# Four graph layers on one core: another order of the node tiles

## The chip, the cores and the metric

The kernel runs on 1 core of one Trainium2 chip. The metric is the device time of one execution in microseconds; before the change it is 1249.79 us, the median of three runs (1248.19 to 1251.66). TensorE is called PE below, VectorE DVE, ScalarE ACT, GpSimd POOL, and SyncE, which only issues DMAs, SP.

## What is computed

Four layers over a graph of 3327 nodes with 512 features. The adjacency matrix is random with about four edges per node, so a layer needs few rows for each node. Each layer adds its result to x:

```python
h = jnp.maximum(_layernorm(x, axis=-1), 0.0)
x = x + _L0_gnn_ref(h, ...)   # relu of [h W_self + b, (mean of the neighbours' h) W_nb + b] W_comb + b
h = jnp.maximum(_layernorm(x, axis=-1), 0.0)
x = x + _L1_gnn_ref(h, ...)   # 8 heads of 64: softmax over the neighbours of leaky_relu(f_src + f_dst), times Wh
h = jnp.maximum(_layernorm(x, axis=-1), 0.0)
x = x + _L2_gnn_ref(h, ...)   # 4 heads of 128 (quaternion weights), then elu
h = jnp.maximum(_layernorm(x, axis=-1), 0.0)
x = x + _L3_gnn_ref(h, ...)   # one head of 512
```

## The kernel before

A first stage (the first quarter of the time) reads the adjacency matrix, makes for each node a list of up to 16 neighbours, counts them, and computes layer 0's projected rows into the DRAM table `T[0]`. It then ranks the nodes by their number of neighbours, most first, and from there on works on tiles of 128 nodes of that ranking. Tile t therefore needs a fixed number of gathered rows for every node of it, `SLOTS[t]`: 15 for tile 0, 8 for tile 1, 7, 7, 6, 6, 6 for tiles 2 to 6, 5 for 7 to 10, 4 for 11 to 15, 3 for 16 to 20, 2 for 21 to 24 and 1 for tile 25, which has 127 nodes; 119 in all. ("A tile with fifteen rows" is meant in this sense; "a row" below is one gathered row for each of the 128 nodes, one indirect DMA.)

`ORDER` (L35) is the order in which every layer goes through the 26 tiles; s is a tile's place in it. All engines run the same order, each its own program:

- POOL (`rows_of`, L1072) issues one indirect DMA per row (L1081) into a ring `GB` of 32 slots. `places` (L89) gives out the slots: it starts again at slot 0 when a tile doesn't fit behind the last one. A slot is written again only when its old row was used (`wait_used`), and tile s waits besides for tile s-8, whose gather semaphore it takes. In layer 0 POOL also gathers each tile's residual row (L1096), in layer 3 it scatters the finished tile to the output (L1111), eight tiles behind the gathers.
- Layer 0: DVE adds the rows of a tile one by one (L1313), each add on the one before, and adds the residual (L1316), round by round, with the norm of the tile before taken between the adds.
- Layers 1 and 2, DVE (L1411): in round r it finishes tile r-3 (L1399 or L1407), normalizes the weights of tile r-1, multiplies that tile's rows with them (`weigh`, L1380; in layer 1 part of the rows are added in pairs, L1392), and takes the first steps of tile r's softmax (`shifted`, L1339 to L1351) and of tile r-3's norm in between. The instructions are in one fixed order, so a wait for tile r's rows at L1339 holds up everything behind it. PE adds the weighed rows of a tile in PSUM with an identity (L703), one sum for each entry of `units`: 94 in layer 1, 119 in layer 2. In PE's round r these sums of tile r-1 alternate with the four steps of tile r-4's projection (L679) in layer 1; what is left over follows behind.
- Layer 3, DVE (L1432): `shifted` of tile r, then the blending of tile r-1 in SBUF (L1460, L1458), each step on the one before; PE transposes the blended tile (L616) and multiplies it with the weights (L749), ACT copies between (L792); DVE adds the product to x (L1440) in round r+3.
- ACT applies the norm (L779), copies the transposed tile to SBUF (L795), takes the exponentials (L845), and copies the projected rows out (L860, L861); SP stores them to the next table (L562).

A node's neighbours may be in any tile, so a layer's first gather waits until the last row of the layer before is stored. `STEP_OF_LAST` is the place of tile 25, the last one in both orders.

Of the kernel before, what the change touches and what calls it, by code (L numbers as in the profile page):

```python
# [31 lines left out]
TILES_WITH = [26, 25, 21, 16, 11, 7, 4, 2, 1, 1, 1, 1, 1, 1, 1]  # L32
SLOTS = [sum(t < n for n in TILES_WITH) for t in range(NT)]
TOTAL = sum(SLOTS)
ORDER = [t for pair in zip([24, 23, 22, 21, 20, 19, 18, 17, 16, 15, 14, 13], [1, 2, 3, 4, 0, 5, 6, 7, 8, 9, 10, 11]) for t in pair] + [12, 25]  # L35
FIRST = [sum(SLOTS[t] for t in ORDER[:s]) for s in range(NT + 1)]
NS = 32

# [3 lines left out]
def units(l, t):  # L42

    pairs = PAIRS[SLOTS[t]] if l == 1 else 0
    return [(2 * k, 2) for k in range(pairs)] + [(k, 1) for k in range(2 * pairs, SLOTS[t])]


def units_ahead(l, s):

    return sum(len(units(i, t)) for i in range(1, l + 1) for t in (ORDER if i < l else ORDER[:s]))  # L50

# [37 lines left out]
def places():  # L89

    base, before, held, at = {}, {}, [None] * NS, 0
    for l in range(4):
        for s, t in enumerate(ORDER):
            if at + SLOTS[t] > NS:
                at = 0
            base[l, s] = at
            for k in range(SLOTS[t]):
                before[l, s, k] = held[at]
                held[at] = (l, s, k)
                at += 1  # L100
    return base, before
# [239 lines left out]
def edges(nc, ctx, g, dr):  # L341
# [85 lines left out]
    BASE, BEFORE = places()  # L427
    STEP_OF_LAST = ORDER.index(NT - 1)
    SETUP = dict(ident=2, xpad=3, mark=7, eight=8, start=9, rowid=10, id=12, upper=14, mrow=16, ones=17, we=18, ones16=19, classes=20, line=21,
# [17 lines left out]
    def wait_gather(e, l, s):  # L447

        e.wait_ge(S[f"gather{s % 8}"], 16 * (l * sum(SLOTS[t] for t in ORDER[s % 8::8]) + sum(SLOTS[t] for t in ORDER[s % 8:s + 1:8])))

    def wait_used(e, l, s, k):
# [4 lines left out]
        elif l < 3:  # L456
            e.wait_ge(S["summed"], units_ahead(l, s) + max(i for i, (first, _) in enumerate(units(l, ORDER[s])) if first <= k) + 1)
        else:
# [1084 lines left out]
```

## Time and profile before

| | |
|---|---|
| median of the runs | 1249.79 us |
| the profiled execution | 1243.5 us, span 1241.8 us |
| PE busy | 897.9 us (72% of the span) |
| DVE busy | 874.3 us (70%) |
| POOL busy | 689.2 us (56%) |
| ACT busy | 394.1 us (32%) |
| chain that ended last | PE 29%, DVE 25%, POOL 16%, DMA 13%, issue 11%, ACT 5% |
| costliest single line of the chain | POOL L1081, the row gathers, 12% |

Busy time is that of an engine over the whole span, not of the path. The chain is what ended last at each moment, followed back from the end; "issue" is time in which an engine waited for nothing that the profile shows. In the time lines a number in brackets is the engine's idle time just before the instruction, with what ended it. A group's mean over the whole run hides that the layers have different limits, so the rows below are of single stretches.

### The profile page before, as it was taken

To read this page: it belongs to the slowest core of one execution; us is meant where nothing else is said; L and a number is where in the kernel's file an instruction comes from. 1 tells how busy PE (TensorE), PEld (TensorE's weight loads), DVE (VectorE), ACT (ScalarE), POOL (GpSimd) and SP (SyncE) were. 2 spreads that over 40 slices of the span, in tenths; PEclk is the share of its full clock that TensorE was granted. 3 is DMA by queue.
4 is the path that set the end of the run, shared out by engine and by line. 5 is a ranking of instruction groups with operands and counts; after the bars stand their busy time and mean duration, and the time that the engine had idled before them with its cause. 6 is when DMAs were issued, how large, how long until landed. Compare 5 with 4: busy or idle time off the path is not lost.

```text
span 1241.8 us, 12157 instructions
## 1 busy us (share of the span) xinstructions
PE 897.9 (72%) x2804; PEld 485.2 (39%) x2804; DVE 874.3 (70%) x2811; ACT 394.1 (32%) x1200; POOL 689.2 (56%) x648
## 2 busy tenths in 40 slices
PE   3985969999256476755999999477888834738674
PEld 1332434444044365542656666234444332313231
DVE  3867699930187698836999897088999945746563
ACT  3552656632023133321323333134354430101110
POOL 4043423365477777617777710377777007777772
PEclk9997989999679689896999999878888966968988
DMA  9999868722678688726757720366677116646662
GB/s 361 387 346 366 316 251 328 224 72 76 200 234 248 181 271 263 238 95 185 202 162 206 209 80 35 95 175 177 188 212 211 53 52 175 171 139 182 181 184 86
DMA packets 81447, 242.74 MB, mean 195 GB/s; under 512 B 16931, under 2 KB 19395, under 8 KB 77275
## 3 DMA queue, kind: packets, MB, share of 16 engines
q0 software_dynamic: 47488, 144.09, 40.1%
q1 hardware_dynamic: 33882, 97.82, 21.4%
q8 instruction: 24, 0.39, 0.1%
q14 instruction: 53, 0.43, 0.1%
HBM read 203.00 MB, written 53.64 MB: 207 GB/s over the span
## 4 chain that ended last, share of the span: by engine, by line
PE 29%; DVE 25%; POOL 16%; DMA 13%; issue 11%; ACT 5%; POOLq 1%; SPq 0%; ACTq 0%
POOL arena L1081 12%; PE psum L679 9%; PE psum L703 7%; PE psum L638 7%; DVE arena L1380 4%; DVE arena L1313 4%; DMA arena<-XV,arena 4%; DVE arena L1192 2%; ACT arena L795 2%; DMA arena<-T,arena 2%; DMA arena<-in_adj 2%; DMA arena<-in_L_gnn_a 2%; DVE arena L1130 2%; DVE arena L1282 2%; PE psum L749 1%
## 5 line engine op out<-in xcount | busy, mean ns | idle before, releaser
L1081 POOL DMA_INDIRECT arena<-T,arena x476 | 518.9, 1090 | 332.9 <-issue 180.3
L703 PE MATMUL psum<-arena,misc 128*128 128x512 f32 x426 | 229.1, 659 | 62.8 <-DVE arena L1380 46.6
L679 PE MATMUL psum<-arena 128*128 128x264 f32 (+1 forms) x832 | 221.1, 412 | 47.3 <-ACT arena L795 47.3
L638 PE MATMUL psum<-arena 128*128 128x512 f32 (+1 forms) x416 | 200.3, 624 | 28.8 <-ACT arena L808 16.4
L679 PEld LDWEIGHTS psum<-arena 128*128 128x128 f32 (+1 forms) x832 | 163.3, 201 | 122.6 <-ACT arena L795 72.3
L616 PE MATMUL psum<-misc,arena 128*128 128x128 f32 (+1 forms) x520 | 87.9, 295 | 145.7 <-ACT arena L779 78.3
L1380 DVE TENSOR_TENSOR arena<-arena 128x512 f32<-128x512 f32 x238 | 160.6, 686 | 1.8
L616 PEld LDWEIGHTS psum<-misc,arena 128*128 128x128 f32 (+1 forms) x520 | 65.4, 152 | 195.8 <-ACT arena L779 89.6
L703 PEld LDWEIGHTS psum<-arena,misc 128*128 128x128 f32 x426 | 82.1, 209 | 146.8 <-issue 100.2
L779 ACT ACTIVATE arena<-arena 128x512 f32<-128x512 f32 x104 | 84.4, 811 | 155.2 <-DVE arena L1289 146.5
L749 PE MATMUL psum<-arena 128*128 128x512 f32 (+1 forms) x208 | 113.2, 695 | 17.9 <-ACT arena L792 17.9
L638 PEld LDWEIGHTS psum<-arena 128*128 128x128 f32 (+1 forms) x416 | 77.7, 198 | 115.0 <-issue 114.0
L1192 DVE FIND_INDEX8 arena<-arena 128x8 uint32<-128x674 f16 x130 | 108.7, 854 | 0.0
L845 ACT ACTIVATE arena<-arena 128x16 f32<-128x16 f32 (+7 forms) x78 | 17.4, 223 | 263.7 <-DVE arena L1351 263.5
L1313 DVE SCALAR_TENSOR_TENSOR arena<-arena 128x512 f32<-128x512 f32 x119 | 88.8, 746 | 16.6 <-DMA arena<-XV,arena 15.5
L1339 DVE TENSOR_TENSOR arena<-arena 128x16 f32<-128x16 f32 (+7 forms) x78 | 14.1, 181 | 118.8 <-DMA arena<-T,arena 118.8
L825 ACT ACTIVATE arena<-arena 128x3330 f16<-128x3330 int32 x26 | 77.4, 2976 | 60.9 <-DVE arena L1192 41.8
L795 ACT ACTIVATE arena<-psum 128x128 f32<-128x128 f32 (+1 forms) x312 | 82.2, 286 | 15.1 <-PE psum L616 15.1
L860 ACT ACTIVATE arena<-psum 128x528 f32<-128x528 f32 (+1 forms) x52 | 31.4, 605 | 133.8 <-PE psum L679 133.8
L749 PEld LDWEIGHTS psum<-arena 128*128 128x128 f32 (+1 forms) x208 | 43.6, 220 | 72.7 <-issue 48.0
L1458 DVE SCALAR_TENSOR_TENSOR arena<-arena 128x512 f32<-128x512 f32 x93 | 70.0, 753 | 1.1
L1130 DVE TENSOR_SCALAR arena<-arena 128x1 f32<-128x1 f32 x234 | 63.6, 272 | 6.8
(138 smaller groups left out, 1006.6 us busy)
## 6 DMA issues: line engine op xcount, KB each, us to landing
arena<-in_adj SPq DMA_DIRECT2D x25, 1663.5 KB, 8.5
T<-arena SPq DMA_DIRECT2D x75, 260.0 KB, 3.6
arena<-T,arena POOLq DMA_INDIRECT x476, 3.8
T<-arena SPq DMA_DIRECT2D x25, 256.0 KB, 2.6
XV<-arena SPq DMA_DIRECT2D x25, 256.0 KB, 2.3
PW<-arena POOLq DMA_DIRECT2D x5, 1024.0 KB, 8.3
arena<-in_x SPq DMA_DIRECT2D x1, 3072.0 KB, 17.6
XV<-arena SPq DMA_DIRECT2D x1, 3072.0 KB, 23.0
```

The lines of the kernel that those rows point to most:

```text
L616: last = e.transpose(p_t[:, k * P:k * P + n], src[0:n, k * P:(k + 1) * P], ident[0:n, 0:n])
L638: last = e.matmul(p_own[which][0:n, :], HT[t % 2][:, k, 0:n], W0[which][:, k, :], start=k == 0, stop=k == 3 and which == 0)
L679: last = e.matmul(p_wh[0:n, a, :], ht[:, k, 0:n], WL[l][:, k, a, :], start=k == 0, stop=k == 3)
L703: e.matmul(p_num[s % 3].rearrange("p (a o) -> p a o", a=2), ident, halves(GB[:, BASE[l, s] + of[n][0], :])[:, :, 0:HALF], start=n == 0, st ...
L749: last = e.matmul(p_num[s % 3][0:n, :], HT[m % 2][:, k, 0:n], W0[0][:, k, :], start=k == 0, stop=k == 3)
L779: e.activation(to[0:n, 0:D], X[0:n, t, :], ACT.Relu, bias=shift[0:n, :], scale=scale[0:n, :]).then_inc(S["h"], 1)
L795: last = e.activation(ht[:, k, 0:n], p_t[:, k * P:k * P + n], ACT.Copy, accum_out=HS[:, k, t:t + 1])
L1081: e.indirect_dma_start(GB[:, BASE[l, s] + k, 0:ROW], None, dr["T"][l], bass.IndirectOffsetOnAxis(ap=(IDP if l else IDX)[:, t, k:k + 1], ax ...
L1130: chain(e.tensor_scalar(t, hv, y, y, ALU.mult, ALU.mult))
L1192: picked = e.max_index(PICK[:, s * 8:s * 8 + 8], EIGHT, MARK[t % 2][:, s * PART:(s + 1) * PART])
L1313: added(e.scalar_tensor_tensor(y, GB[:, base + k, 0:D], SHARE[:, t, k:k + 1], y if k else xv[:, 0:D], ALU.mult, ALU.add))
L1380: return e.tensor_tensor(both, both, p, ALU.mult)
```

## The change

Only the constant `ORDER` changes. `FIRST`, the places in the ring, the gather semaphores (s modulo 8) and every engine's program follow from it; the first stage does not use it.

```diff
-ORDER = [t for pair in zip([24, 23, 22, 21, 20, 19, 18, 17, 16, 15, 14, 13], [1, 2, 3, 4, 0, 5, 6, 7, 8, 9, 10, 11]) for t in pair] + [12, 25]
+ORDER = [24, 23, 22] + [t for pair in zip([1, 2, 3, 4, 5, 6, 7, 8, 9, 10], [21, 20, 19, 18, 17, 16, 15, 14, 13, 12]) for t in pair] + [0, 11, 25]
```

In rows per tile the order is, before and after:

```
before 2 8 2 7 2 7 2 6 3 15 3 6 3 6 3 5 3 5 4 5 4 5 4 4 4 1
after  2 2 2 8 2 7 3 7 3 6 3 6 3 6 3 5 4 5 4 5 4 5 4 15 4 1
```

Tile 0 has slots 9 to 23 of the ring before, and 13 to 27 after.

## Rows read from the trace of the kernel before

**Rows 1.** Groups by line, POOL, stretches 323:521 (first two) and 1021:1211

```profile
L1081 POOL DMA_INDIRECT arena<-T,arena x119 | 126.3, 1062 | 60.6 <-issue 58.1 <-DVE arena L1313 2.4
L1096 POOL DMA_INDIRECT arena<-XV,arena x26 | 27.6, 1060 | 7.9 <-issue 6.7 <-DVE arena L1313 0.9 <-DVE arena L1316 0.3
...
L1081 POOL DMA_INDIRECT arena<-T,arena x119 | 128.7, 1082 | 95.2 <-DMA T<-arena 59.2 <-issue 35.0 <-DVE arena L1460 0.6
```

**Rows 2.** Stretches: length, PE, PEld, DVE, ACT, POOL busy (count), PE clock, DMA, GB/s

```profile
323.60:551.60 228.00, 133.72 (x538) 100.17 (x538) 165.74 (x466) 66.26 (x288) 153.95 (x146) 0.85 0.72 220
...
643.40:766.90 123.50, 115.56 (x424) 73.13 (x423) 114.41 (x410) 41.18 (x191) 58.73 (x53) 1.00 0.49 145
...
823.70:1007.60 183.90, 151.90 (x512) 80.07 (x513) 172.97 (x609) 79.46 (x343) 109.47 (x97) 0.89 0.55 160
...
1021.70:1229.00 207.30, 130.09 (x312) 56.35 (x312) 122.21 (x353) 20.89 (x52) 155.65 (x144) 0.83 0.57 167
```

**Rows 3.** Time line, layer 0, tile 0: start us, us, instruction, [idle before]

```profile
408.43 1.01 POOL L1081 DMA_INDIRECT arena<-T,arena  x1 [0.30 <-issue]
...
410.57 0.18 DVE L1307 TENSOR_TENSOR arena<-arena 128x15 uint32<-128x15 f32 x1 [10.45 <-DMA arena<-T,arena]
...
420.60 1.28 POOL L1081 DMA_INDIRECT arena<-T,arena  x1 [0.30 <-issue]
...
443.14 0.17 ACT L861 ACTIVATE arena<-psum 128x8 f32<-128x8 f32 x1
```

**Rows 4.** Time line, end of layer 0

```profile
519.90 1.50 POOL L1096 DMA_INDIRECT arena<-XV,arena  x1 [0.30 <-issue]
...
539.98 0.17 ACT L861 ACTIVATE arena<-psum 128x8 f32<-128x8 f32 x1
...
545.61 0.17 ACT L861 ACTIVATE arena<-psum 127x8 f32<-127x8 f32 x1
```

**Rows 5.** Time line, layer 1: tiles at places 1, 3 and 9; sums of tile 0

```profile
567.35 0.23 DVE L1339 TENSOR_TENSOR arena<-arena 128x64 f32<-128x64 f32 x1 [8.75 <-DMA arena<-T,arena]
...
579.96 0.21 DVE L1339 TENSOR_TENSOR arena<-arena 128x56 f32<-128x56 f32 x1
...
626.86 0.28 DVE L1339 TENSOR_TENSOR arena<-arena 128x120 f32<-128x120 f32 x1 [2.07 <-DMA arena<-T,arena]
...
643.18 6.17 PE L703 MATMUL psum<-arena,misc 128*128 128x512 f32 x14
```

**Rows 6.** Time line, layer 2, DVE: shifts at places 1, 3, 9; round starts

```profile
808.89 0.19 DVE L1339 TENSOR_TENSOR arena<-arena 128x32 f32<-128x32 f32 x1 [8.73 <-DMA arena<-T,arena]
...
821.34 0.19 DVE L1339 TENSOR_TENSOR arena<-arena 128x28 f32<-128x28 f32 x1 [0.91 <-DMA arena<-T,arena]
...
823.72 0.69 DVE L1407 SCALAR_TENSOR_TENSOR arena<-arena 128x512 f32<-128x512 f32 x1
...
832.47 0.69 DVE L1407 SCALAR_TENSOR_TENSOR arena<-arena 128x512 f32<-128x512 f32 x1
...
838.25 0.69 DVE L1407 SCALAR_TENSOR_TENSOR arena<-arena 128x512 f32<-128x512 f32 x1
...
869.36 0.22 DVE L1339 TENSOR_TENSOR arena<-arena 128x60 f32<-128x60 f32 x1 [4.82 <-DMA arena<-T,arena]
```

**Rows 7.** Time line, layer 3: tile 0, then the end

```profile
1096.18 1.01 POOL L1081 DMA_INDIRECT arena<-T,arena  x1 [0.30 <-issue]
...
1119.21 5.93 PE L749 MATMUL psum<-arena 128*128 128x512 f32 x8 [0.69 <-ACT arena L792]
...
1125.19 0.69 DVE L1440 TENSOR_TENSOR arena<-arena,psum 128x512 f32<-128x512 f32 x1 [4.33 <-PE psum L749]
...
1208.81 1.03 POOL L1081 DMA_INDIRECT arena<-T,arena  x1 [0.30 <-issue]
...
1224.30 3.70 PE L749 MATMUL psum<-arena 128*127 128x512 f32 x8 [0.68 <-ACT arena L792]
...
1228.04 0.69 DVE L1440 TENSOR_TENSOR arena<-arena,psum 127x512 f32<-127x512 f32 x1 [4.13 <-PE psum L749]
```

## The prediction

> **What bounds the kernel now.** I began with the chain of waits: it changes its engine from layer to layer, so one share for the whole run says little. What precedes the first row gather (323.6 us, the start of the first stretch in [rows 2]) goes by tile number and does not see the order. I then read each layer's throughput, and last the time line at the places of tile 0 and at each layer's ends.
>
> Layers 0 and 3 are bound by the issue of row gathers on POOL. In layer 0 POOL is busy 126.3 + 27.6 us and idle only 60.6 + 7.9 us, nearly all "issue" (0.30 before each, and 24 us ahead of the very first); in layer 3 it is likewise, apart from the 59 us ahead of its first [rows 1]. Hence 145 issues start between 323.6 and 519.9 without a hole [rows 2, 4]: 196.3 / 144 = 1.36 us each. Layer 3 has 136 (119 rows, 17 stores) from 1021.7 to the last row's at 1208.8 [rows 2, 7]: 187.1 / 135 = 1.39 each. When the heavy tile comes, DVE has nothing else to do: in layer 0 it waits 10.45 us for tile 0's rows [rows 3]. Layer 1 is bound by PE (115.6 of 123.5 us busy, granted clock 1.00, in its later part), layer 2 by DVE (173.0 of 183.9) [rows 2]; there POOL runs ahead and only the start and tile 0's place make them wait [rows 5, 6].
>
> **The change part by part.** Nothing is added or removed: 119 gathered rows a layer, 94 sums in layer 1, the same tiles. Moved are (a) the start, 2, 2, 2, 8 rows in place of 2, 8, 2, 7; (b) tile 0, from tenth to last but two, followed by tiles of 4 and 1 rows; (c) the slots of the ring and the eight gather semaphores, which follow the order. Sums are made against the profiled execution.
>
> *Layer 0, end.* The last POOL issue starts at 519.90 [rows 4]. In the new order the last issues are tile 0's 15 rows, its residual gather, four rows, a gather, one row, a gather: tile 0's last row is the ninth from the end, so it starts at 519.90 - 8 x 1.36 = 509.0 and ends at 510.0. One correction: beside tile 0's chained adds an issue takes 1.28 us in place of 1.01 [rows 3]; six stood there, 1.6 us, and those adds now fall behind the row in question: 508.4. Before, tile 0's last row ended at 409.4 and its own new row was ready at 443.3 [rows 3]: 33.9 us of DVE, ACT and PE work that nothing follows faster. The tile behind it now has four rows in place of three, +0.7; the last two tiles follow at 5.63 us each, as at the end now [rows 4]. Layer 0 ends at 508.4 + 33.9 + 0.7 + 11.3 = 554.3 against 545.8 [rows 4]: **+8.5**. Bounds: +5 (the low clock after the pause gone and the last tiles overlapping more) and +10 (no correction).
>
> *Layer 1, start.* The third and later tiles' first results wait for the shift of the fourth tile, since DVE takes its steps in order (round r holds the end of tile r-3 and the shift of tile r). Now the fourth tile's shift is at 579.96, after 19 rows; ten rows had landed at 567.35 [rows 5]. Fourteen rows have landed four issues later, 567.35 + 4 x 1.31 = 572.6: 7.4 earlier. From there PE works without a hole, at 6.17 / 7 = 0.88 us a sum [rows 5]. It has one more sum left over from the 8-row tile and, after the next two tiles, three fewer sums behind it than before (2+2+2+6+2 against 2+6+2+5+2): -0.9 and -2.6. Where tile 0 stood PE lost 2.1 us with DVE waiting for its rows [rows 5]; these return, less a little, say 1.4. Sum: -7.4 + 0.9 + 2.6 - 1.4 = **-5.3**. At the end tile 0's eleven sums meet a PE that has more queued than DVE: it is, by my estimate, a round (8 us) behind, so DVE's round of about 16 us (15 rows and four pair sums at 0.69, some 3 fixed) ends before PE's 11 x 0.88 + 5 and what it had left over, and costs nothing; were PE not behind, up to 5. Bounds -10 and 0.
>
> *Layer 2.* The same start: 808.89 + 4 x 1.31 = 814.1 against 821.34, 7.2 earlier [rows 6]. DVE then never stops. A round costs 8.75 us for seven rows and 5.78 for two [rows 6], 0.6 a row, so order does not matter; but six more rows are still to be weighed at that point (113 against 107): -3.6 given back. The wait of 4.82 at tile 0 goes [rows 6]. Sum: -7.2 + 3.6 - 4.8 = **-8.4**. What is late next? Fresh rows: the eighth tile (33 rows) has landed 23 issues after the tenth row, 808.89 + 23 x 1.38 = 840.6, and DVE asks for it near 843 (823.7 - 7.2, rounds of 9.4, 5.8 and 8.8, and 2.4 within the next); close, but from there DVE needs 14.7 us for a pair of tiles and POOL under 13. Bounds -11 and -5.
>
> *Layer 3, end.* The last row's issue starts at 1208.81 [rows 7]. Tile 0's last row will be the seventh before it (a store, four rows, a store, then that row): 7 x 1.39 = 9.7, so it starts at 1199.1, and 1.6 us less, as in layer 0, for the issues that tile 0's blending slowed: 1197.5. Before, it started at 1096.18 and the tile was added into the residual at 1125.19 [rows 7], 29.0 later; 1.3 for the fourth row of the tile that DVE asks for ahead of the blending; then two tiles at 4.82 (0.69 for an add and 4.13 of wait, [rows 7]). The last add comes at 1197.5 + 29.0 + 1.3 + 9.6 = 1237.4 against 1228.04: **+9.4**. Bounds +6 and +11.5.
>
> *Ring.* Tile 0 takes slots 13 to 27, over tiles that stand four to eight places ahead of it. In layers 0 and 3 the row it needs free last was issued some 30 issues (41 us) before; in layers 1 and 2 it is freed three rounds (22 us) before DVE asks. I cost it at nothing; cover gone, POOL would fetch these 15 rows late, up to 15 x 1.38 = 21 us less what DVE does meanwhile.
>
> **Sum:** 8.5 - 5.3 - 8.4 + 9.4 = **+4.2 us**, 1243.5 to 1247.7 on the profiled execution. That one lies 0.5% below the median of the runs; against the median 1249.8 it is 1254.0.
>
> The Trainium skill bears on the two corrections (1.6 us each). The rows show gathers' issues slowed beside DVE operations with two operands in SBUF [rows 3]. "SBUF — State Buffer", section "Who interferes with whom", has such a DVE operation contend only with a GpSimd instruction that reads SBUF, and infers that descriptor generation needs the write side, so it would leave them alone. By that rule there is no correction and the sum would be +7.4; by the row it is +4.2. The row is of this kernel, and it decides.
>
> **The rivals.**
> *Faster: POOL speeds up when DVE rests.* Layers 0 and 3 are POOL's, and an issue takes 1.06 and 1.08 us in the mean against 1.01 alone [rows 1, 3]: an excess of 145 x 0.05 + 136 x 0.07 = 17 us. If the new order, with light and heavy tiles evenly paired, frees half of it (8.5 us), the sum is -4.3: 1245.5. It decides once the mean issue in those layers falls below 1.03. For it: the excess is real. Against it: the same DVE work still lies beside the same issues.
> *No change: the tails are cheap.* After the pause for tile 0 PE's clock is low: eight matmuls take 5.93 us where they take 3.70 at the very end [rows 7]. If PE keeps its clock through the new pause, each tail is 2.2 shorter: -0.2, 1249.6. Against it: the pause is as long as the one in the trace. The same no-change comes if the layer 1 start is worth its full 7.4 and 2.1.
> *Much slower: the ring.* If POOL stands before tile 0's slots in layers 1 and 2, half of both gains goes, and 2 to 4 us at each end on top: +14, 1264. Against it: POOL's idle time in layer 0 is 0.30 us times its issues and little else [rows 1].
>
> **How the numbers follow.** Measured against no change, this kernel can tell about 0.3%, 3.75 us. Forecast 0.50, its own range 1250.5 to 1258 (0.36 beyond the bound, 0.14 within it); no change 0.20; faster 0.18; ring 0.12. Hence faster 0.18, same 0.34, slower 0.48. The four terms' bounds lie some 3 us to a side each, some 6 together if they err independently: 1248 to 1260. I widen that to 1246, nearly the faster rival's time, and to 1261; the ring's 1264 stays out.
>
> **What the new profile would show.** Right: layer 0 ends 9 us later, layers 1 and 2 last 5 and 8 us less, layer 3's last add is 9 later after its first gather; DVE waits over 10 us for a gather at tile 0's new place in layers 0 and 3 and hardly at all in 1 and 2; POOL's last row at the old distance from the layer's start. Wrong: a tail below 5 us (then something of tile 0's work overlaps), a layer 1 that gains its full start (PE was not the bound), POOL gaps over 0.35 us (the ring), or mean issue times that move.

## The result: 0.4% slower, close to the forecast

The changed kernel takes 1252.62 us (median of 11 runs, 1249.03 to 1255.78), the kernel before in the same comparison 1247.24 (11 runs, 1245.23 to 1251.66): a ratio of 1.004 with a 95% interval of 1.0025 to 1.0055. The profiled execution took 1250.74 us, its span is 1249.0. Forecast were 1254.0 us and, as a difference, +4.2; the medians differ by 5.4, the two profiled executions by 7.2 (1250.74 against 1243.5).

First the groups by line on POOL, layer 0 and then layer 3, as in [rows 1]:

```profile
L1081 POOL DMA_INDIRECT arena<-T,arena x119 | 126.3, 1062 | 60.6 <-issue 57.9 <-DVE arena L1313 2.4 <-DVE arena L1316 0.3
L1096 POOL DMA_INDIRECT arena<-XV,arena x26 | 27.0, 1040 | 7.9 <-issue 7.6 <-DVE arena L1313 0.3
...
L1081 POOL DMA_INDIRECT arena<-T,arena x119 | 127.7, 1073 | 89.4 <-DMA T<-arena 53.4 <-issue 34.7 <-DVE arena L1460 1.2
```

POOL issues the same gathers in the same time; idle before them is again 0.30 us each. Then the stretches, as in [rows 2] (length; PE, PEld, DVE, ACT, POOL busy; granted clock; DMA share; GB/s):

```profile
324.90:562.10 237.20, 142.96 (x538) 106.78 (x538) 166.30 (x465) 66.23 (x288) 153.35 (x145) 0.82 0.69 211
...
652.50:775.90 123.40, 115.69 (x428) 73.77 (x426) 116.12 (x394) 39.74 (x184) 59.23 (x54) 1.00 0.47 133
824.10:1004.00 179.90, 152.54 (x516) 77.05 (x517) 173.88 (x608) 77.69 (x335) 110.69 (x100) 0.93 0.60 169
1018.40:1235.50 217.10, 135.08 (x312) 57.86 (x312) 122.45 (x353) 20.88 (x52) 153.97 (x144) 0.82 0.56 159
```

Layer 0 went from 228.0 to 237.2 us up to the next first gather with POOL's work unchanged. DVE in layer 2 is now busy 173.9 of 179.9 us, where it was 173.0 of 183.9. The time line of layer 0, tile 0 at its new place and the end, answers to [rows 3, 4]:

```profile
510.64 1.00 POOL L1081 DMA_INDIRECT arena<-T,arena  x1 [0.30 <-issue]
...
512.76 0.18 DVE L1307 TENSOR_TENSOR arena<-arena 128x15 uint32<-128x15 f32 x1 [11.77 <-DMA arena<-T,arena]
...
516.38 0.75 DVE L1313 SCALAR_TENSOR_TENSOR arena<-arena 128x512 f32<-128x512 f32 x1 [2.83 <-DMA arena<-XV,arena]
...
521.11 1.00 POOL L1096 DMA_INDIRECT arena<-XV,arena  x1 [0.30 <-issue]
...
544.92 0.17 ACT L861 ACTIVATE arena<-psum 128x8 f32<-128x8 f32 x1
...
550.54 0.17 ACT L861 ACTIVATE arena<-psum 128x8 f32<-128x8 f32 x1
...
556.16 0.17 ACT L861 ACTIVATE arena<-psum 127x8 f32<-127x8 f32 x1
```

POOL's last issue stands 196.2 us after the layer's first, as before (196.3). The eight issues behind tile 0's last row take 1.00 or 1.01 us each, though tile 0's adds run from 516.38 on. Tile 0's last row ends 9.5 us ahead of that issue, and its own new row is copied out 33.5 us later, with two tiles still to follow, 5.62 us each. Layer 1, the fourth tile's shift and then tile 0's, beside [rows 5]:

```profile
583.10 0.23 DVE L1339 TENSOR_TENSOR arena<-arena 128x64 f32<-128x64 f32 x1 [5.81 <-DMA arena<-T,arena]
...
737.68 0.27 DVE L1339 TENSOR_TENSOR arena<-arena 128x120 f32<-128x120 f32 x1
```

Layer 2, the same two, beside [rows 6]:

```profile
819.62 0.19 DVE L1339 TENSOR_TENSOR arena<-arena 128x32 f32<-128x32 f32 x1 [5.95 <-DMA arena<-T,arena]
...
966.77 0.21 DVE L1339 TENSOR_TENSOR arena<-arena 128x60 f32<-128x60 f32 x1
```

The fourth tile's shift comes 21.0 us after layer 1's first gather (562.1) where it came 28.4 after it, and 21.5 in place of 28.0 in layer 2 (first gather at 798.16). Tile 0's shift has no wait any more. POOL, however, stands still once before the last of tile 0's 15 rows in layer 1, for a ring slot that PE's sums have yet to free:

```profile
720.74 1.11 POOL L1081 DMA_INDIRECT arena<-T,arena  x1 [1.31 <-PE psum L703]
```

It costs nothing, since DVE asks for the tile only at 737.68. Layer 3, beside [rows 7]:

```profile
1194.29 1.01 POOL L1081 DMA_INDIRECT arena<-T,arena  x1 [0.30 <-issue]
...
1196.43 0.18 DVE L1339 TENSOR_TENSOR arena<-arena 128x15 f32<-128x15 f32 x1 [13.89 <-DMA arena<-T,arena]
...
1204.96 0.16 DVE L1339 TENSOR_TENSOR arena<-arena 128x4 f32<-128x4 f32 x1 [4.19 <-DMA arena<-T,arena]
...
1219.39 6.38 PE L749 MATMUL psum<-arena 128*128 128x512 f32 x8 [0.69 <-ACT arena L792]
...
1225.81 0.69 DVE L1440 TENSOR_TENSOR arena<-arena,psum 128x512 f32<-128x512 f32 x1 [4.07 <-PE psum L749]
...
1230.63 0.69 DVE L1440 TENSOR_TENSOR arena<-arena,psum 128x512 f32<-128x512 f32 x1 [3.16 <-PE psum L749]
...
1235.45 0.69 DVE L1440 TENSOR_TENSOR arena<-arena,psum 127x512 f32<-127x512 f32 x1 [4.13 <-PE psum L749]
```

Tile 0's adding into x comes 31.5 us after its last row's issue, where it came 29.0 after it, and two tiles follow at 4.82. POOL's last row of layer 3 is issued 185.5 us after the first, where it was 187.1.

### The profile page after: what moved, and what is told of

Same layout as the page of the kernel before. It is cut to its first block, busy times and chain, and to the rows that moved or that the text cites. A ratio compares the mean times of both kernels' runs of the same rounds, so it can differ in the third digit from the quotient of the medians.

```text
span 1249.0 us, 12157 instructions
## 1 busy us (share of the span) xinstructions
PE 906.9 (73%) x2804; PEld 489.4 (39%) x2804; DVE 877.9 (70%) x2811; ACT 394.5 (32%) x1200; POOL 683.8 (55%) x648
## 4 chain that ended last, share of the span: by engine, by line
PE 26%; DVE 25%; POOL 19%; issue 13%; DMA 12%; ACT 4%; POOLq 1%; SPq 0%; ACTq 0%
POOL arena L1081 14%; PE psum L679 9%; PE psum L638 7%; DVE arena L1380 6%; PE psum L703 5%; DMA arena<-XV,arena 3%; DVE arena L1313 3%; ACT arena L795 2%; DVE arena L1192 2%; DMA arena<-T,arena 2%; DMA arena<-in_adj 2%; DMA arena<-in_L_gnn_a 2%; DVE arena L1130 2%; DVE arena L1282 2%; DVE arena L1407 1%
## 5 line engine op out<-in xcount | busy, mean ns | idle before, releaser
L679 PE MATMUL psum<-arena 128*128 128x264 f32 (+1 forms) x832 | 230.3, 424 | 47.4 <-ACT arena L795 47.4
L703 PE MATMUL psum<-arena,misc 128*128 128x512 f32 x426 | 223.2, 639 | 42.8 <-DVE arena L1380 40.3
L638 PE MATMUL psum<-arena 128*128 128x512 f32 (+1 forms) x416 | 199.5, 622 | 29.1 <-ACT arena L808 16.3
L679 PEld LDWEIGHTS psum<-arena 128*128 128x128 f32 (+1 forms) x832 | 169.5, 209 | 127.4 <-ACT arena L795 73.5
L749 PE MATMUL psum<-arena 128*128 128x512 f32 (+1 forms) x208 | 117.7, 719 | 17.8 <-ACT arena L792 17.8
L703 PEld LDWEIGHTS psum<-arena,misc 128*128 128x128 f32 x426 | 78.3, 202 | 122.8 <-issue 73.9
L638 PEld LDWEIGHTS psum<-arena 128*128 128x128 f32 (+1 forms) x416 | 77.3, 197 | 115.2 <-issue 114.1
L1313 DVE SCALAR_TENSOR_TENSOR arena<-arena 128x512 f32<-128x512 f32 x119 | 88.8, 746 | 21.9 <-DMA arena<-XV,arena 21.1
L749 PEld LDWEIGHTS psum<-arena 128*128 128x128 f32 (+1 forms) x208 | 45.2, 228 | 75.3 <-issue 50.6
L1458 DVE SCALAR_TENSOR_TENSOR arena<-arena 128x512 f32<-128x512 f32 x93 | 70.0, 753 | 1.1
```

The lines of the kernel that those rows point to most:

```text
L638: last = e.matmul(p_own[which][0:n, :], HT[t % 2][:, k, 0:n], W0[which][:, k, :], start=k == 0, stop=k == 3 and which == 0)
L679: last = e.matmul(p_wh[0:n, a, :], ht[:, k, 0:n], WL[l][:, k, a, :], start=k == 0, stop=k == 3)
L703: e.matmul(p_num[s % 3].rearrange("p (a o) -> p a o", a=2), ident, halves(GB[:, BASE[l, s] + of[n][0], :])[:, :, 0:HALF], start=n == 0, st ...
L749: last = e.matmul(p_num[s % 3][0:n, :], HT[m % 2][:, k, 0:n], W0[0][:, k, :], start=k == 0, stop=k == 3)
L1313: added(e.scalar_tensor_tensor(y, GB[:, base + k, 0:D], SHARE[:, t, k:k + 1], y if k else xv[:, 0:D], ALU.mult, ALU.add))
```

## The experiments

In most of them each layer has an order of its own: every use of `ORDER` becomes `ORDERS[l]`, and places and semaphore counts follow. All times are in us; "layer" is the time from a layer's first gather to its last new row copied out (layer 3: to its last add into x), from the profiled execution.

**Four orders on a slow chip.** The first four kernels ran on a chip where the kernel before took 1400.38 (7 runs, 1386.56 to 1405.74), 12% more than on any other chip used here. They are compared within it.

```diff
-ORDER = [...]
+ORDERS = [BEFORE_ORDER, AFTER_ORDER, AFTER_ORDER, BEFORE_ORDER]   # mid_heavy
+ORDERS = [AFTER_ORDER, BEFORE_ORDER, BEFORE_ORDER, AFTER_ORDER]   # ends_heavy
+ORDER = [24, 23, 22, 1, 21, 2, 20, 3, 19, 0, 18, 4, ..., 12, 10, 11, 25]  # light_start
+ORDER = [24, 1, 23, 2, 22, 3, ..., 15, 10, 14, 11, 13, 0, 12, 25]         # late_heavy
```

mid_heavy. 

> Layers 0 and 3 go through the tiles in the old order, layers 1 and 2 in the new one. Theory (each layer's change stands by itself: the two ends cost, the two starts give): layers 0 and 3 keep the length of the kernel before, 222.2 us from the first gather to the last copied row and 206.3 us from the first gather to the last add; layers 1 and 2 keep the changed kernel's 230.5 and 212.0. Sum 13.3 us below the kernel before, a ratio of 0.989. Rival (the ring and the gather semaphores carry a layer's order into the next one, so a part of the gain is only there when all layers share an order): less than 8 us faster, with POOL gaps at the first eight tiles of layers 1 and 3.

ends_heavy. 

> The reverse: layers 0 and 3 in the new order, layers 1 and 2 in the old one. Theory: layer 0 231.4 and layer 3 217.1 us as in the changed kernel, layers 1 and 2 236.2 and 219.6 as before; 20 us above the kernel before, a ratio of 1.016. Rival (the losses of layers 0 and 3 belong to the shared order): under 12 us slower.

light_start. 

> The changed kernel's start (2, 2, 2, 8 rows and so on) in all layers, but tile 0 at the tenth place as before. Theory: layers 0 and 3 as before (222 and 206 us), since only what stands behind the last gather counts there; layers 1 and 2 start 7 us earlier, but tile 0's rows, now numbers 37 to 51 in place of 40 to 54, land only 3 x 1.38 = 4.1 us earlier, so that its wait grows and about 2 to 4 us are left in each: 5 us faster in all, 0.996. Rival (the start is worth its full 4 us in layer 1 and 4 in layer 2 and the wait at tile 0 stays at 2.1 and 4.8): 8 us faster, DVE's wait for tile 0 unchanged.

late_heavy. 

> The old start (2, 8, 2, 7) in all layers, tile 0 at the last place but two. Theory: the ends cost what they cost in the changed kernel, 9.2 us in layer 0 and 10.8 in layer 3; of the layers between only the waits for tile 0 come back, 1.4 and 4.8: 13.8 us slower, 1.011. Rival (the start had a part in layers 0 and 3 too): those two layers come out under 228 and 213 us.

Measured, 4 runs each: mid_heavy 1367.33, ratio 0.975 (0.968 to 0.982); ends_heavy 1380.87, 0.987 (0.981 to 0.994); light_start 1386.78, 0.991 (0.986 to 0.997); late_heavy 1362.74, 0.976 (0.969 to 0.982). The signs for ends_heavy and late_heavy are the wrong way round. In layer 3 a late tile 0 gave 227.0 and 228.3, a tenth one 237.1 and 239.4. What differs is seen in the waits of late_heavy (total, times, longest), ACT's first and then PE's:

```profile
ACT arena L860 <- remote: 108.4, 11, 22.7
ACT arena L792 <- remote: 73.1, 6, 20.4
...
PE psum L679 <- issue: 47.6, 12, 13.3
PE psum L749 <- issue: 42.9, 11, 14.0
```

Single engines stand still for up to 23 us with nothing shown that they wait for, while their instructions keep their durations (L749 717 ns in the mean, 719 in the kernel after). In the profile before, ACT has 6.4 us put down to "issue" and none to "remote", and PE none of either. POOL has holes too (one of 10.8 us in layer 0 of late_heavy). On this chip the issue of gathers no longer bounds layers 0 and 3, so these four say little about the forecast; what holds the engines up stays open.

**The same on a chip of usual speed.** Here the kernel before took 1248.03 (13 runs, 1244.99 to 1255.21).

mid_heavy_2. 

> The same kernel as mid_heavy (the new order in layers 1 and 2, the old one in layers 0 and 3), since that run fell on a chip where the kernel before took 1400 us and engines stood still for 5 to 14 us with nothing shown ahead of them. If this chip runs the kernel before near 1247 us: theory (the places of the tiles cost by layer, as the two profiled runs show) layer 0 near 222 us from its first gather, layer 1 near 230.5, layer 2 near 212, layer 3 near 206; ratio 0.989 (-13 us). Rival (layers are not independent: what layers 1 and 2 gain is there only since layers 0 and 3 end late): layers 1 and 2 as in the kernel before, ratio 1.000. If this chip is slow as well, ratio 0.975 again.

ends_heavy_2. 

> The same kernel as ends_heavy (the new order in layers 0 and 3 alone). If the kernel before takes about 1247 us here: theory layer 0 near 231, layer 3 near 217, layers 1 and 2 near 236 and 220 as in the kernel before; ratio 1.016 (+20 us). Rival (POOL's contention is relieved, or the ends are not additive): under 1.008. If this chip is slow as the last one, ratio 0.987 again, with the order of the sign turned round.

mid_heavy_2 took 1235.48 (4 runs), ratio 0.989 (0.984 to 0.993), ends_heavy_2 1265.12 (4 runs), ratio 1.013 (1.010 to 1.016). The two differences, -12.6 and +17.1 us, add up to +4.5, where the whole change made 5.4: the layers are independent within the noise, and the theory holds for both signs, though the ends cost less than the 20 us expected of them. With the repeats there are several profiled executions of each layer in either order:

| layer | old order | new order | difference | predicted |
|---|---|---|---|---|
| 0 | 222.2, 224.7, 221.5, 223.4 | 231.4, 230.3, 231.3 | +8.0 | +8.5 |
| 1 | 236.2, 236.3, 236.1 | 230.5, 230.8, 230.9 | -5.5 | -5.3 |
| 2 | 219.7, 220.3, 219.7 | 212.1, 212.3, 212.2 | -7.7 | -8.4 |
| 3 | 206.4, 204.6, 208.8, 206.7, 204.2 | 217.1, 217.1 | +11.0 | +9.4 |

The sum is +5.8, against 5.4 between the medians. (The profiled executions of the two kernels alone, on which the forecast was made, give +9.3, -5.7, -7.6 and +10.7.) Layers 1 and 2 repeat within 0.6 us; in the old order 0 and 3 repeat only within 3 and 5. (The columns hold, without the slow chip, before, after, and those of the kernels here and below whose layer is in that order; busy_pe and narrow_adds without the layer that they alter.)

**The light start alone.**

```diff
+START_ORDER = [24, 23, 22, 1, 21, 2, 20, 3, 19, 0, 18, 4, ..., 12, 10, 11, 25]
+ORDERS = [BEFORE_ORDER, START_ORDER, START_ORDER, BEFORE_ORDER]
```

> Layers 0 and 3 in the old order; layers 1 and 2 begin with 24, 23, 22, 1 as in the new order, but tile 0 stays tenth. It parts the light start from tile 0's new place, which together gave 0.989 (layer 1 -5.4, layer 2 -7.4 in mid_heavy_2 against the profile before). Theory (the prediction's terms): layer 1 -7.4 + 0.9 + 2.6 = -3.9, layer 2 -7.2 + 3.6 = -3.6, DVE's waits for tile 0's rows (2.1 lost on PE in layer 1, 4.8 in layer 2) stay; ratio 0.994. Rival (the light start is all of it, the wait at tile 0 is given back later anyway): 0.989. Rival the other way (the start is given back, tile 0's place is what gains): 0.998 or above.

1243.08 (10 runs) against 1247.50, ratio 0.996 (0.993 to 0.999). Layer 1 takes 233.8 and layer 2 217.7: the start is worth -2.4 and -2.2 against the means of the table, not -3.9 and -3.6, and tile 0's place the rest, -3.1 and -5.5. The fourth tile's shift stands 21.1 and 21.6 after the layer's first gather, as early as in the kernel after: of the 7.3 and 6.4 us that the starts gain, 4.9 and 4.2 are given back. In layer 1 a part of that is lost where tile 0 stands. Its shift in start_only, where the kernel before waited 2.07 us [rows 5]:

```profile
626.34 0.28 DVE L1341 TENSOR_TENSOR arena<-arena 128x120 f32<-128x120 f32 x1 [4.05 <-DMA arena<-T,arena]
```

DVE gets there 5.2 us earlier than before, tile 0's rows only 3.2 us earlier, so the wait grows by 2.0; the theory had it stay. In layer 2 it does stay (4.68 against 4.82). The start's worth and that of tile 0's place are therefore not independent in layer 1: the late place also takes away the wait that the early start adds.

**A lighter start.**

```diff
+LIGHT_ORDER = [24, 23, 22, 21, 20, 1, 19, 2, 18, 3, ..., 13, 8, 12, 9, 10, 0, 11, 25]
+ORDERS = [BEFORE_ORDER, LIGHT_ORDER, LIGHT_ORDER, BEFORE_ORDER]
```

> mid_heavy with layers 1 and 2 begun lighter still: 24, 23, 22, 21, 20, 1, 19, 2, ... 9, 10, 0, 11, 25, so that the fourth tile has two rows in place of eight. Theory (the start of a layer waits for the fourth tile's rows, one gather each 1.31 us): DVE's first full round starts 6 x 1.31 = 7.9 us earlier; given back are 4 sums at 0.88 in layer 1 (3.5) and 6 rows at 0.6 in layer 2 (3.6). So layer 1 is near 226, layer 2 near 208, ratio to the kernel before 0.982 (mid_heavy 0.989). Rival (the layers are bound by their engines from the start on, the start is not what gained): same as mid_heavy, 0.989. Second rival (fresh rows run out, since the light tiles use rounds of DVE faster than POOL fills them): DVE waits over 5 us for gathers in layers 1 and 2 and the ratio is 0.989 or above.

1224.07 (4 runs) against 1248.03, ratio 0.981 (0.977 to 0.984): the theory's 0.982. Layer 1 took 224.5 (226 expected), layer 2 207.7 (208), and POOL's longest hole in them is 0.5. DVE waits 3.7 and 1.4 us at the sixth tile, less than the second rival's 5. PE's mean granted clock in the 40 us that start 20 us after layer 1's first gather was 1.00, against 0.87 in the kernel after; no sum here holds that, and it may be a part of the 1.5 us beyond the forecast. This version is faster than both kernels.

**PE kept at work before tile 0's product.** The kernel after, with this in layer 3:

```diff
+            if SLOTS[t] == 15:
+                for _ in range(10):
+                    e.matmul(psum[:, 6, :], ident, W0[1][:, 0, :], start=True, stop=True)
             e.wait_ge(S["blended"], FIRST[s + 1])
```

> The kernel after, with ten more 128x512 matmuls into an unused bank of PSUM ahead of PE's wait for tile 0's blending in layer 3 (about 4 us of work that nothing reads), so that PE has worked shortly before it must multiply tile 0. Theory (PE's granted clock is low after its pause, which costs every late tail about 2.2 us): the eight 128x512 matmuls for tile 0 take 3.7 us in place of 5.9 and layer 3 is 2.2 us shorter (215 in place of 217), ratio to the kernel before 1.002 to 1.003 where the kernel after has 1.004. Rival (the clock doesn't hang on this, or the ten matmuls end too early before the real ones): 5.9 us as before and 1.004. A second one: PE gets to the real ones late, layer 3 longer by up to 4 us.

1249.34 (10 runs) against 1248.03, ratio 1.001 (0.999 to 1.003), where the kernel after has 1.004 (1.0025 to 1.0055); the two intervals overlap a little. Layer 3 took 214.6, 2.5 less. The windows of tile 0's eight matmuls and of the next tile's, the clock third from the end, first in the kernel after:

```profile
1219.39:1225.77 6.38, 6.38 (x10) 2.75 (x11) 2.35 (x6) 0.20 (x1) 0.51 (x1) 0.57 0.11 41
1226.90:1230.60 3.70, 3.70 (x10) 1.74 (x11) 0.54 (x2) 0.00 (x0) 1.02 (x1) 1.00 0.19 71
```

and in busy_pe:

```profile
1218.61:1223.79 5.18, 5.18 (x10) 2.38 (x11) 2.81 (x7) 0.20 (x1) 0.96 (x1) 0.71 0.13 51
1224.91:1228.60 3.69, 3.69 (x10) 1.73 (x11) 0.55 (x2) 0.00 (x0) 1.03 (x1) 1.00 0.19 71
```

These two executions alone would say that the added work raised the clock from 0.57, near the lower of its two levels (1.2 of 2.4 GHz), to 0.71, and took 1.2 us off the product. But ends_heavy_2 runs layer 3 in the same order without added work, and there tile 0's product has this window:

```profile
1233.92:1239.38 5.46, 5.46 (x10) 2.39 (x11) 2.36 (x6) 0.20 (x1) 0.50 (x1) 0.67 0.13 48
```

The product's clock varies that much by itself, so that the added work changed it is not shown. What differs from both is the four transposes just ahead of the product, 0.66 us in busy_pe, 1.12 and 1.11 without the added work. From the issue of tile 0's last row to its add into x busy_pe takes 29.9 us, the other two 31.5 and 30.6; the row itself is issued 175.0 us after the layer's first, against 175.9 and 176.8. So 0.7 to 1.6 us of the layer's 2.5 lie in the tail, and the rest in POOL's issues, which the edit does not touch. Neither the theory (3.7 us) nor the rival (5.9) came out. The ten matmuls took 8.75 us and not about 4 (0.88 each, the price of one of PE's sums in [rows 5]) and ended 1.9 us before the transposes. Shown is what the low clock costs: the same eight matmuls take 5.18 to 6.38 us at a mean granted clock of 0.71 to 0.57, and 3.70 at 1.00.

**Narrow adds.** The kernel before; this leaves out most of layer 0's sums of neighbours.

```diff
+                    w = 8 if k else D
-  added(e.scalar_tensor_tensor(y, GB[:, base + k, 0:D], SHARE[...], y if k else xv[:, 0:D], ...))
+  added(e.scalar_tensor_tensor(y[:, 0:w], GB[:, base + k, 0:w], SHARE[...], y[:, 0:w] if k else xv[:, 0:D], ...))
```

> The kernel before, with all adds of layer 0 but each tile's first made 8 columns wide in place of 512 (this leaves out most of layer 0's sums of neighbours, everything else is as it was). The question is whether the chained adds of DVE lengthen POOL's issue of a gather. Theory (they do, as the rows of tile 0 show, 1.28 against 1.01 us): the mean issue in layer 0 falls from 1.06 to about 1.01, the last gather ends about 7 us earlier after the first (189 in place of 196), layer 0 is 7 us or more shorter (DVE is shorter at its end too). Rival (the long issues come from something else, such as a queue or other transfers): mean issue stays at 1.05 to 1.07 and the last gather at 195 to 197.

The theory fell. The time was 1242.36 (10 runs) against 1247.50, ratio 0.996 (0.994 to 0.999), with layer 0 at 219.9, some 2 to 3 us shorter, where 7 or more were expected. The group of POOL's gathers in layer 0 comes first; then, from the time line, the five gathers beside tile 0's adds, which took 1.41, 1.28, 1.27, 1.28 and 1.27 before ([rows 3] has one):

```profile
L1081 POOL DMA_INDIRECT arena<-T,arena x119 | 125.5, 1054 | 60.4 <-issue 57.1 <-DVE arena L1314 2.7 <-DVE arena L1317 0.6
```

```profile
415.08 1.01 POOL L1081 DMA_INDIRECT arena<-T,arena  x1 [0.30 <-issue]
416.39 1.43 POOL L1081 DMA_INDIRECT arena<-T,arena  x1 [0.30 <-issue]
418.13 1.07 POOL L1081 DMA_INDIRECT arena<-T,arena  x1 [0.30 <-issue]
419.51 1.01 POOL L1081 DMA_INDIRECT arena<-T,arena  x1 [0.30 <-issue]
...
422.27 1.00 POOL L1081 DMA_INDIRECT arena<-T,arena  x1 [0.30 <-issue]
```

At this one place most of the long issues go, 6.5 us for the five before and 5.5 now. That 1 us is all that the 119 gathers gain: their mean falls from 1062 ns to 1054, and the last one ends after 195.5 us in place of 196.0. The rest of the layer's gain lies behind it, where DVE's adds are shorter (24.4 us in place of 26.2 to the last new row); the median fell by more than the layer, and where the remainder comes from isn't known. Elsewhere in layer 0 issues are as long as before beside adds of 8 columns; what lengthens them isn't known. Layer 3 was not tested. There, in the kernel before, 31 of the 119 gathers take over 1.15 us, and 77% of their time lies beside DVE's chained 128x512 steps (L1458), against 19% for the other 88. That is an association, not yet a cause.

**A light tile last but one, and then none at the end.**

```diff
+ENDS_ORDER = [23, 1, 22, 2, 21, 3, 20, 4, 19, 0, 18, 5, ..., 13, 10, 12, 11, 24, 25]
+ORDERS = [ENDS_ORDER, LIGHT_ORDER, LIGHT_ORDER, ENDS_ORDER]                     # ends_light
+ENDS_ORDER = [24, 1, 23, 2, 22, 3, 21, 4, 20, 25, 0, 19, 5, ..., 10, 13, 11, 12]
+LIGHT_ORDER = [25, 24, 23, 22, 21, 1, 20, 2, ..., 13, 9, 12, 0, 10, 11]         # last_early
```

ends_light. 

> light_mid, and in layers 0 and 3 a two-row tile is moved from the first place to the last but one (23, 1, 22, 2, 21, 3, 20, 4, 19, 0, ..., 10, 12, 11, 24, 25), so that the last tiles are light while the starts, bound by POOL alone, are not to suffer. Theory (in these layers only what follows the last gathers counts): DVE has two adds of 0.75 fewer ahead of the last tile, 1 to 2 us less in each of the two layers; ratio to the kernel before 0.979 (light_mid 0.981). Rival (PE and the distance between the last rows, 5.6 and 4.8 us, set the end): 0.981. Rival: tile 0, which is no longer tenth but has the same place behind heavier tiles, or the ring's slots make POOL wait: above 0.983.

1230.14 (4 runs) against 1247.50, ratio 0.983 (0.978 to 0.989): the gain expected did not come. The interval overlaps light_mid's, but both end layers are longer in the profile, 225.5 and 210.5 against 223.4 and 204.2. The time line of ends_light, layer 3, last gather and last adds into x:

```profile
1189.75 1.27 POOL L1084 DMA_INDIRECT arena<-T,arena  x1 [0.30 <-issue]
...
1198.76 0.69 DVE L1443 TENSOR_TENSOR arena<-arena,psum 128x512 f32<-128x512 f32 x1 [0.45 <-PE psum L752]
...
1203.58 0.69 DVE L1443 TENSOR_TENSOR arena<-arena,psum 128x512 f32<-128x512 f32 x1 [1.84 <-PE psum L752]
...
1208.40 0.69 DVE L1443 TENSOR_TENSOR arena<-arena,psum 128x512 f32<-128x512 f32 x1 [3.16 <-PE psum L752]
...
1213.22 0.69 DVE L1443 TENSOR_TENSOR arena<-arena,psum 127x512 f32<-127x512 f32 x1 [4.13 <-PE psum L752]
```

The last tiles of four, two and one rows all come at 4.82 us. POOL fills a two-row tile in three issues, some 4 us, so it only adds to the queue in front of PE: the last add comes 22.2 us after the last gather's end, in light_mid 18.2. The other 2.3 of the 6.3 us between the two layers lie in POOL's issues ahead of it. From this the last kernel was made.

last_early. 

> light_mid with the one-row tile 25 taken from the last place: in layers 0 and 3 it stands ahead of tile 0 (24, 1, 23, 2, 22, 3, 21, 4, 20, 25, 0, 19, 5, ..., 11, 12), in layers 1 and 2 it is the first (25, 24, 23, 22, 21, 1, 20, 2, ..., 13, 9, 12, 0, 10, 11). Theory, from ends_light (a tile takes 5.6 us in layer 0 and 4.8 in layer 3 from one result to the next however few rows it has, so a tile lighter than POOL fills in that time only prolongs the end): in light_mid tile 25 is done 25.7 us (layer 0) and 18.9 us (layer 3) after its last row, tile 12 22.7 and 16.7; with tile 12 last the ends come 3.0 and 2.2 us earlier. In layers 1 and 2 one row fewer stands ahead of the fourth tile, 1.3 us each. Together -8 us: ratio to the kernel before 0.974 (light_mid 0.981). Rival (four rows at the very end cost DVE what one did not, the gain is lost to their adds, or layer 1 and 2 lose it at their ends): 0.981. Rival: the seat ahead of tile 0 takes time from POOL or lets the ring wait: above 0.981.

```profile
1182.29 1.27 POOL L1083 DMA_INDIRECT arena<-T,arena  x1 [0.30 <-issue]
...
1199.73 0.69 DVE L1442 TENSOR_TENSOR arena<-arena,psum 128x512 f32<-128x512 f32 x1 [4.14 <-PE psum L751]
```

1215.31 (5 runs, 1212.54 to 1219.24) against 1247.89 (9 runs), ratio 0.975 (0.972 to 0.977), where the theory had 0.974. The last add comes 16.2 us after the last gather's end. The layers take 221.5, 222.1, 206.5 and 203.0, that is 1.9, 2.4, 1.2 and 1.2 less than in light_mid (3.0, 1.3, 1.3 and 2.2 expected). In layers 0 and 3 that is within what they vary between runs; the clearer sign is layer 3's tail, 18.2 us before and 16.2 now, where 2.2 less were expected. It is the fastest version of the study, by order alone.

## Why the prediction was right, step by step

*The whole.* +4.2 was forecast and 5.4 measured, slower by 0.4%; the sign of all four terms and what makes them (POOL's issue ahead of an exposed tail in layers 0 and 3, the start and the wait at tile 0 in 1 and 2) hold, shown by the two kernels that carry half of the change each and by start_only. Single terms inside them were off by 1 to 2 us and cancelled in part, so that the sum came within 1.2 us is luck to that extent.

*Layer 0, +8.5; measured +8.0 (+9.3 between the two profiled executions).* Two errors cancelled. The correction of 1.6 for issues slowed by tile 0's adds was wrong here: the last row of tile 0 ended at 186.7 us after the first gather, where the sum without the correction has 186.4 and with it 184.8. The tail of 45.9 was 44.7. The forecast took the six slow issues beside tile 0's adds to fall behind its last row. But the eight issues behind that row took 1.00 or 1.01 us each, and the excess over that, 7.6 us in all of the layer's issues but the last (7.7 before), now lay ahead of the row. narrow_adds agrees: adds of 512 columns account for about 1 us of it. "SBUF — State Buffer" of the Trainium skill, section "Who interferes with whom", would leave descriptor generation alone beside such adds. Over a layer the trace is near to that (1054 against 1062 ns); at tile 0's place it is not, and the section alone would not have told one from the other. By that rule the sum was +7.4, too high by 2.0; as recorded, too low by 1.2.

*Layer 1, -5.3; measured -5.5.* The start gained what was said (28.4 to 21.0), but start_only shows -2.4 for it, net, where the steps gave -3.9. Tile 0's place brought -3.1, not -1.4. The forecast's two parts were each off by 1.5 or so, in opposite directions, and their sum came out by that luck. What it had wrong is that the wait at tile 0 stays at 2.1 us when the start alone moves: it grows to 4.05, as DVE gains on POOL, and the late place takes all of it away. Whether the sums given back (3.5) were mis-sized as well these runs do not part. As forecast, tile 0's eleven sums at the end cost nothing that shows.

*Layer 2, -8.4; measured -7.7.* The start gained 6.5 of 7.2 and kept 2.2 of 3.6; tile 0's place brought 5.5, 4.8 of it the wait that was read from the trace. Nothing was late next: in layers 1 and 2 DVE waits for rows at no shift after the fourth.

*Layer 3, +9.4; measured +11.0.* Tile 0's last row was issued 175.9 us after the first gather, 175.8 forecast; but it is 176.8 and 175.0 in ends_heavy_2 and busy_pe, whose order here is the same, so the hit does not prove the correction of 1.6. The tail was longer by 1.3: 0.5 since the next tile's rows landed later than one more row explains (1204.96 - 1194.29 = 10.7 against 8.9, of which 1.3 was counted), and 0.5 on PE, whose eight matmuls took 6.38 and not 5.93; the rest is open.

*The ring and the rivals.* POOL has one hole over the prediction's 0.35 us, the 1.31 us at tile 0's last row in layer 1 (busy_pe and mid_heavy_2 have it too). It is the ring's doing, and nothing waits for it. POOL didn't speed up: the mean issue in layers 0 and 3 went from 1062 and 1082 ns to 1062 and 1073, far from 1.03. The clock rival fell: PE's granted clock was low at tile 0's product after the new pause too (0.57), and the tail did not get shorter by it.

## What to carry to other kernels

Read which engine bounds each stage before ordering its tiles: where the issue of gathers does, the heavy tile should come early, since what follows its last row is exposed (+8 and +11 us here), and a very last tile that takes about as long to fetch as to compute did better than the lightest (layer 3's tail 16.2 us against 18.2); where an engine computes nearly throughout, begin with the lightest tiles and leave the heavy one for late. One order for all four layers made these two cancel; an order by layer gave 2.5%. A start that is 7 us earlier was worth only 2 net, so price what is still to be done at that moment and the waits that grow when one engine gains on another. And compare two executions of the same order before putting a difference of 1 us in one of them down to an edit.

## What was not expected of the hardware

- One of the chips ran the same program at 1400 us in place of 1247, its engines standing still for up to 23 us with no shown reason; the ratio of ends_heavy was 0.987 there and 1.013 elsewhere. A comparison of orders holds only for chips in the same condition.
- At tile 0's place five gathers that took 1.27 to 1.41 us beside wide chained adds took 1.00 to 1.07 beside narrow ones, but for one of 1.43, and yet the mean of the layer's 119 moved by 8 ns.
- The same eight matmuls, with PE idle for 9.1 and 10.0 us ahead of their transposes, took 6.38 us at a mean granted clock of 0.57 in one execution and 5.46 at 0.67 in another, though the two kernels' layer 3 is the same; 8.75 us of added matmuls that ended 1.9 us ahead of the transposes left the product at 5.18 (0.71).
